# Two more turns by DMA in a macaron block: y of phase 15 and u of phase 2

## What is computed

```python
x = x + 0.5 * ffn(layernorm(x))
x = x + attn(layernorm(x))
x = x + 0.5 * ffn(layernorm(x))
...
# attn
xf = concatenate([u[:, :1], einsum('btd,ed->bte', u[:, 1:], WB)])
xb = concatenate([einsum('btd,ed->bte', u[:, 1:], WBf), u[:, -1:]])
gamma = sigmoid(xf @ w1.T + xb @ w2.T + b)
y = gamma * (xf + xb) + (1.0 - gamma) * u
...
# ffn: 64 experts with 64 hidden features each, top 8 of a token, and one shared expert
shared = silu(xf @ Ws_up) @ Ws_down
aff = xf @ centroids.T
_, idx = top_k(aff + expert_biases, 8)
w = sigmoid(take_along_axis(aff, idx));  w = w / (sum(w) + 1e-08)
h = silu(einsum('td,edf->etf', xf, W_up))
y = einsum('etf,efd->etd', h, W_down)
routed = einsum('etd,te->td', y, cw)
```

## Time and profile before

| what | value |
| --- | --- |
| median of three runs | 777.49 us (776.26 to 778.57) |
| the profiled execution | 776.51 us |
| its span | 774.7 us |
| granted TensorE clock | 1.00 of full speed, mean over the span |
| TensorE busy | 764.2 us |
| VectorE, ScalarE, GpSimd busy | 630.8, 629.0, 526.2 us |
| DMA moved | 21.99 MB, mean 28 GB/s |

### The profile page before, as it was taken

How to read it: one execution, slowest core, us unless ns; L and a number is a source line. 1 busy time by engine, 2 the same in 40 slices (tenths; PEclk the granted TensorE clock), 3 DMA queues, 4 the chain that set the end, 5 groups by cost and what they waited for, 6 DMA issues and landing times.

```text
span 774.7 us, 12422 instructions
## 1 busy us (share of the span) xinstructions
PE 764.2 (99%) x3509; PEld 630.0 (81%) x3509; DVE 630.8 (81%) x1388; ACT 629.0 (81%) x1222; POOL 526.2 (68%) x534
## 2 busy tenths in 40 slices
PE   7999999999999999999999999999999999999998
PEld 6777877888888888888888888888888888888786
DVE  6787989888797787977979788887888788797875
ACT  7987777787887888878888679887788887786885
POOL 4785655676778776776777678776786776564453
PEclk9999999999999999999999999999999999999999
DMA  8000000010101101002010021011110110100000
GB/s 291 15 1 14 15 1 1 14 41 28 28 15 28 41 27 41 14 14 59 22 27 14 16 65 27 14 27 27 40 27 14 27 28 27 14 1 1 14 1 14
DMA packets 56541, 21.99 MB, mean 28 GB/s; under 512 B 42816, under 2 KB 55360, under 8 KB 56512
## 3 DMA queue, kind: packets, MB, share of 16 engines
q1 hardware_dynamic: 56512, 21.64, 10.7%
HBM read 9.05 MB, written 2.10 MB: 14 GB/s over the span
## 4 chain that ended last, share of the span: by engine, by line
PE 89%; DVE 4%; ACT 4%; POOL 1%; issue 0%; DVEq 0%
PE y_ps L979 14%; PE y_ps L981 14%; PE y_ps L980 14%; PE up L979 14%; PE up L981 14%; PE up L980 14%; PE side L997 2%; ACT g_hi L625 1%; ACT up L591 1%; PE side L1030 1%; PE side L1029 1%; POOL g_lo L415 1%; PE y_ps L975 1%; DVE gated L833 1%; DVE up L833 1%; DVE g_lo L842 1%
## 5 line engine op out<-in xcount | busy, mean ns | idle before, releaser
L415 POOL TENSOR_TENSOR g_lo<-gated,g_hi 128x512 fp32r<-128x512 f32 x256 | 333.9, 1305 | 190.8 <-ACT g_hi L625 189.8
L591 ACT ACTIVATE up<-up 128x512 f32<-128x512 f32 x513 | 300.4, 586 | 61.9 <-PE up L981 60.1
L833 DVE TENSOR_TENSOR gated<-up,cw 128x512 f32<-128x512 f32 x256 | 175.7, 686 | 82.4 <-ACT up L591 73.4
L979 PE MATMUL y_ps<-g_hi,wd_hi 128*128 128x512 f32 x512 | 202.4, 395 | 1.6 <-POOL g_lo L415 1.6
L979 PE MATMUL up<-x_hi,wu_hi 128*128 128x512 f32 x512 | 200.2, 391 | 1.0 <-DVE g_lo L842 0.9
L981 PE MATMUL y_ps<-g_hi,wd_lo 128*128 128x512 f32 x512 | 199.6, 390 | 0.0
L981 PE MATMUL up<-x_hi,wu_lo 128*128 128x512 f32 x512 | 199.4, 390 | 0.0
L980 PE MATMUL y_ps<-g_lo,wd_hi 128*128 128x512 f32 x512 | 199.4, 389 | 0.0
L980 PE MATMUL up<-x_lo,wu_hi 128*128 128x512 f32 x512 | 199.4, 389 | 0.0
L833 DVE TENSOR_TENSOR up<-up,cw 128x512 f32<-128x512 f32 x256 | 176.7, 690 | 20.1 <-ACT up L591 18.1
L625 ACT CAST g_hi<-up 128x512 fp32r<-128x512 f32 x256 | 150.6, 588 | 46.5 <-DVE up L833 45.8
(11 more groups left out here) (141 smaller groups left out, 558.8 us busy)
## 6 DMA issues: line engine op xcount, KB each, us to landing
x_in<-in_x SPq DMA_DIRECT2D x8, 256.0 KB, 2.7
wu_raw<-in_w_up SPq DMA_DIRECT2D x4, 512.0 KB, 7.9
wd_raw<-in_w_down SPq DMA_DIRECT2D x4, 512.0 KB, 8.6
x_res<-in_x SPq DMA_DIRECT2D x8, 256.0 KB, 2.6
out<-out_sb SPq DMA_DIRECT2D x7, 256.0 KB, 2.2
mix<-in_mix SPq DMA_DIRECT2D x1, 389.0 KB, 7.3
n_turned_halves<-n_halves SPq DMA_TRANSPOSE x17, 2.7
out<-out_sb SPq DMA_DIRECT2D x2, 128.0 KB, 1.9
```

Of the source, the lines that this page charges most:

```text
L415: nc.gpsimd.tensor_tensor(g_lo[:, i, :], gated[:, t // 2 % ORING, :], g_hi[:, i, :].bitcast(fp32), ALU.subtract).then_inc(lo_done[1], 1)
L591: nc.scalar.activation(up[i][:, :], up[i][:, :], ACT.Silu).then_inc(silu_done, 1)
L833: nc.vector.tensor_tensor(gated[:, t // 2 % ORING, :] if t % 2 else up[i][:, :], up[i][:, :], cw[ph.q][:, :], ALU.mult).then_inc(gate_done, 1)
L979: nc.tensor.matmul(o, a[0], b[0], start=start, stop=False)
```

## The change

- Phase 15 turns the y of phase 14 by DMA: ScalarE's copy writes halves, SyncE issues one turn more (`turn_y(2 * B - 1)`), GpSimd joins in slots 5 and 7, adds x2 in slot 9 (before, VectorE did in slot 4) and keeps x2 in slot 13 instead of 11.
- Phase 2 turns its u by DMA: packs in slots 17 and 19, one turn more on SyncE ahead of that of the weights, joins in 22 and 23, in place of four transposes and three copies by ScalarE in slot 22.
- The layernorm of x1 stands earlier (statistics 9 and 10, rstd 12, norm 13 and 15), attention a slot later (26), the weights' packs in 24 and 25 and joins in 29 and 30, statistics and rstd of x2 a slot later (30, 31 and 32).
- Semaphore counts follow.

```diff
 AT_THIRD = {
     "x_split": 3, "aff": 7, "sig": 9, "bias": 8, "max": 9, "take": 9,
-    "gate": 9, "sum": 9, "inv": 15, "cw_pack": (17, 21), "cw_join": (25, 27),
-    "y_t": 6, "x1": 8, "stat1": (10, 12), "aggr1": 13, "rstd1": 14, "norm1": (16, 18), "xu": 19, "u_t": 22,
-    "u_copy": 22, "attn": 25, "tanh": 25, "gamma": 25, "x2": (27, 28),
-    "stat2": (29, 30), "aggr2": 30, "rstd2": 31, "norm2": (33, 34), "x2_pack": (33, 34),
+    "gate": 9, "sum": 9, "inv": 15, "cw_pack": (24, 25), "cw_join": (29, 30),
+    "y_t": 6, "x1": 8, "stat1": (9, 10), "aggr1": 11, "rstd1": 12, "norm1": (13, 15), "u_pack": (17, 19), "xu": 21, "u_join": (22, 23),
+    "attn": 26, "tanh": 26, "gamma": 26, "x2": (28, 29),
+    "stat2": (30, 31), "aggr2": 31, "rstd2": 32, "norm2": (33, 34), "x2_pack": (33, 34),
     "late": 3,
 }
...
 AT_LAST = {
-    "y_t": 4,
-    "out": 4, "keep": 11, "late": 2,
+    "y_join": (5, 7), "sum_out": 9, "keep": 13, "late": 2,
 }
...
             def turn_u(c):
-                hold(sp, u_packed, c - 1)
+                hold(sp, u_packed, c)
...
             turn_x(2)
+            turn_u(1)
             turn_weights(2)
...
             turn_weights(2 * B - 3)
+            turn_y(2 * B - 1)
             store(B - 2)
...
             def join_u(c, h):
                 if h == 0:
-                    hold(pool, u_moved, 16 * (c - 1))
+                    hold(pool, u_moved, 16 * c)
...
-                    hold(pool, y_moved, 16 * (ph.p - 2))
+                    hold(pool, y_moved, 16 * (ph.p - 2 - (ph.late is not None)))
...
             def u_copy(c):
-                act.wait_ge(u_turned, min(c, 2) + 1)
+                act.wait_ge(u_turned, min(c, 1) + 1)
...
                     if not ph.first:
-                        y_copy(ph.p)
+                        y_copy(ph.p, ph.y_dma)
```

## The result

The changed kernel takes **779.63 us** (median of 10 runs, 779.09 to 780.18), the kernel before, on the same chip, 777.85 (10 runs, 776.23 to 778.59): ratio 1.0027, interval 1.0018 to 1.0035. It is a little slower. The profiled executions stand 2.9 us apart: 779.38 us with a span of 777.6, against 776.51 and 774.7. Why the medians differ by a microsecond less is taken up in the last experiment.

A forecast was written before the change was run, and what follows sets the result against it. TensorE, busy 764.2 of 774.7 us, was taken as the bound. Terms -0.44 + 0.0 + 2.1 + 0.0 + 0 + 1.0 = +2.7 on 776.5 gave 779.2, plus 1.0 for the median: 780.2, range 777.2 to 781.6.

The forecast's parts named there:

- The u turn: Phase 2: four transposes and the longer gap behind them leave TensorE, -0.44 us.
- The y turn: Phase 15: the -0.8 us won is lost waiting for GpSimd's low part of tile 1, net 0.0 us.
- The middle: Phase 2, layernorm of u moved up: TensorE waits before up products 19 and 21, +2.1 us.
- the two bounds: w_norm in phase 2: lower 0.42 us unheld, upper 1.4 us held like w_sel; the upper was taken.
- Attention a slot later: Phase 2: TensorE reaches attention at 150.0, GpSimd is ready at 150.2; 0.0 us, bounds 0 and +0.4.
- The weights behind u: Phase 2: two packs and two joins move to gaps of the same kind, first read in phase 3; 0 us.
- The end of phase 2: rstd2 behind tile 31's low part delays the norm of x2 and the product opening y_ps in phase 3, +1.0 us.
- The base of the sum: Whole kernel: profiled execution 776.5 us, with the median of three runs, 777.5, taken as 1.0 above it.
- w_norm free: Rival, phase 2: w_norm isn't held, the middle costs 1.0, in all +1.6 us, 779.1; chance 0.22.
- The race at rstd1: Rival, phase 2: VectorE gets in before GpSimd, sum -0.44 or -1.2 us, 776.7, not slower; chance 0.13.
- The joins of u: Rival, phase 2: joins late by 0.4, two waits empty the ring; +3.5 to +4.5 us, 781.5; chance 0.07.
- The end of the phase alone: Rival, phase 2: only its end waits, the middle keeps its 0.44; +0.6 us, 778.1; chance 0.08.

The follow-up runs named there:

- the last experiment: The kernel before, unchanged, profiled twice more to look at its two groups of times: 778.97 and 776.48 us.
- all five kernels of the table: The change (779.63 us) and, against it, norm's first half a slot later (779.21), three entries moved (777.61), w_norm in slot 12 (778.65), norm on ScalarE (777.45).
- Moving three entries at once: Changed kernel with w_inv and w_norm in slot 12, norm of x1 in 14 and 15, x2 and its statistics a slot earlier: 777.61 us, ratio 1.0002.
- the better of the two single moves: Changed kernel with w_inv and w_norm in slot 12 instead of 15: 778.65 us; the other, norm of x1 in slots 14 and 15: 779.21 us.

## Why the prediction was right, and where it wasn't

The forecast was 780.2, the time is 779.63; the sum was +2.7, the profiled spans give +2.9. Step by step:

- **The u turn, -0.44.** Right: products behind the turn's place come 0.42 to 0.44 nearer in all five kernels of the table.
- **The y turn, 0.0.** Right, for the reason given: the wait is for tile 1's low part, 0.62 us from start to start (0.7 named). What I concluded from it for the experiments fell: I took the turn's 0.8 for a gain that this one low part gave back. With the low part moved away, 0.09 is all that shows, because the low part of tile 2 is met next.
- **The middle, +2.1.** Measured 2.06 at up product 22, with both waits at the products named. From start to start the first is 0.76 us (0.75), the second 1.04 (1.2), and the product behind each comes another 0.13 and 0.15 later (0.1 taken). The second half of the norm took 0.60, as replayed. w_norm took 1.31 us: of the two bounds the upper was the right one. By the Trainium skill, "SBUF — State Buffer", Who interferes with whom, a VectorE instruction with two SBUF inputs waits for the whole of a GpSimd one that reads SBUF and was issued first. This trace agrees (0.42 alone, 1.31 beside).
- **Attention a slot later, 0.0.** Wrong in size, within its bounds: it cost 0.22 (from +1.64 to +1.86 in the table). My 7.4 us of work for GpSimd against the 7.2 that it had was that close, and I rounded it to nothing. In the trace GpSimd needs 7.43 us (142.34 to 149.77), and TensorE's first product of attention starts at 149.87, 0.19 late.
- **The weights behind u, 0.** No wait in phase 3 names them.
- **The end of phase 2, +1.0.** Right: 1.14 at the opening of y_ps (7.03 against 5.89), 1.19 in the phase's length, and 1.08 of it is gone with rstd2 back in its place. The path was the one named, but over half of the wait (0.61) is met one step earlier, before up product 5.
- **The base of the sum.** This step failed. I set the median, 777.5, over the profiled run, 776.5, and carried the 1.0 us between them over to the changed kernel. That microsecond was no overhead of every execution: it comes of the kernel before's upper group of times, and the changed kernel's ten runs show none. Against 776.5 plus 2.9 its 779.63 leaves 0.2. So the terms were 0.2 too low and the base 0.8 too high, and that the forecast came out within 0.6 owes a little to the two having opposite signs. The ratio of the medians, 1.0027, understates what the change does to an undisturbed execution (2.9 of 776.5, 0.37%).

The rivals: w_norm free would have left phase 2's middle a microsecond cheaper, and it wasn't free. The race at rstd1 was lost by VectorE, as in the earlier trace rows. The joins of u did cost something, 0.2. The end of the phase alone would have been one of three waits.

## What to carry to other kernels

Moving a step by a slot on an in-order engine isn't priced by its own duration but by what it then stands beside. Replay the two engines against each other and look which instruction starts inside which; here w_norm, whose own slot wasn't changed, went from 0.42 us to 1.31 because what stands before it moved. Moving three entries at once gave phase 2 less (-0.86) than the better of the two single moves that touch it (-1.13). Taking the norm off VectorE gave the most (-1.69), but a four-column operation left there was held for 1.25 us, and 0.3 us was lost again by way of ScalarE's queue. Before comparing medians, look whether a kernel's times form groups, and in which stretch of the trace these differ.

## What the runs showed of the hardware

- Four VectorE instructions with two SBUF tensors as inputs, held by a GpSimd tensor-tensor operation of 1.29 us, end behind it by their own length less 0.13 to 0.14 us, as if they began their work only then: `shift` (0.15 alone, 1.25 held) 0.02 behind, w_norm (0.42, 1.31) 0.29 behind, w_dup and x1 (0.69, 1.62 and 1.63) 0.55 behind. How early in the GpSimd instruction one starts matters more than how much it has to do.
- The order is settled anew for each instruction, and a start shown slightly earlier doesn't win it: of two norms of 0.33 us one that began 0.09 us before a low part was held to 1.46; where a pair began 0.21 us before one, the first took 0.33 and the second 1.34, so that GpSimd came in between.
- Taking an instruction away from GpSimd's queue brought the next one forward by 7.6 us (x_lo from 120.13 to 112.52) and cost 0.9 us in all.
- The turn of y in phase 4 landed 3.6, 3.7 and 4.3 us after its issue in three profiled executions (2.7 to 3.1 in the others), and phase 4 was 1.2 to 1.9 us longer in just these. Turns that landed after up to 4.7 us in phases 3 and 13 cost nothing.
